# Another order of the q, k and value products, moves one a step, and maxima 13 steps ahead, in a 24-unit attention kernel on one core

## Chip, core and metric

The kernel runs on one core of a Trainium2 chip. The metric is the time of one execution on the device, in microseconds. A profile is one more execution of the same program, recorded by the hardware profiler.

## What is computed

The input x has 4 batches of 1024 tokens with 128 channels, in fp32. Two layers are added to it one after the other, each on a normalised x. The first is a time-mixing layer: three projections, a scan over the tokens (wkv), a gate and a projection back. The second is a chain of six attention cells per batch. Cut to its core:

```python
for c in range(NUM_NOD):                      # 6 cells
    nsrc = min(c + 1, MAX_PREV)
    snode = c - nsrc
    in_q, in_k, in_v = (c - 1, snode, snode + nsrc // 2)
    q = ew[c, 0] * (nodes[in_q] @ We[eq] + be[eq])
    k = ew[c, 1] * (nodes[in_k] @ We[ek] + be[ek])
    v = ew[c, 2] * (nodes[in_v] @ We[ev] + be[ev])
    o = _mha(q, k, v, Wq[c], Wk[c], Wv[c], Wo[c])   # 8 heads of 16 channels, softmax over 1024 keys
    nodes[c] = act_w[c] * o + q
    lind += nsrc
out = _layernorm(nodes[NUM_NOD - 1], ln_g, ln_b)
```

A cell takes q from the cell before it, k and v from older cells. The batches do not depend on each other.

## The kernel before

**Units and steps.** One cell of one batch is a unit, so there are 24. `BATCH_OF` sets their order, with at least three units from a cell to the next of the same batch. A unit has 32 steps: 4 groups (4 heads by 512 queries) of 8 steps, one per 128 keys. Steps are numbered through, s from 0 to 767; r is the step within its unit. In a step TensorE makes

- 4 scores (L496), 128 keys by 512 queries each, into one of three `ring` banks. ScalarE puts exp of each into `e_ring` (L792);
- 2 maxima (`maxima`, L522), 128 queries by 1024 keys each, into the two `wide` buffers in turn, 14 steps (`LOOKAHEAD`) ahead of the scores. Each is reduced by VectorE to one negated maximum per query (L1040). A score and half of a maximum run side by side;
- the weighted sum of values for the step before (`weighted`, L544), in two halves, or in one piece in the second half of a step that also has a product.

Before it writes a wide buffer again, TensorE waits for VectorE to have reduced what was in it:

```python
if w >= 2:
    e.wait_ge(v_mx, w - 1)
```

**The combine.** When the 16 maxima of a group are there (`finished(s)`), VectorE splits them in a high and a low part and transposes them, ahead of the reductions of that step: L1045, L1049 (both tensor_tensor on `max_neg` and `max_part`, in SBUF) and L1058. With `LOOKAHEAD` 14 this is at the start of steps r = 2, 10, 18 and 26. SyncE stores the result to DRAM (`store_rows`) and a step later loads it as extra rows of `q_aug` (`load_rows`), so that the score matmul subtracts the maximum.

**Products.** Some steps hold one product more, in their first half, into a ring bank (`product_of`): two halves of k (`head_k`), of q (`head_q`), of the values (`project_v`) for a coming unit, and two of the output of the unit before (`project_out`, L466 and L471). They stand at r = 1 (q), 5 and 9 (k), 13 and 17 (output), 21 and 25 (values) and 30 (q). ScalarE evicts k, q and output, VectorE copies the values (L935). In the two units after a batch's last cell has run, steps 18 and 19 hold the turns of its result (`final_turn`).

**GpSimd.** Each half of k and of q is split into a rounded high part (cast, L1141) and the rest (tensor_tensor, L1143), both on SBUF. When a part is complete, six DMAs issued by GpSimd (`move_part`, L287) copy it into `q_aug` or `k_aug`; q's go one a step, r = 3 to 8, k's go in two threes at r = 10 and 11. Each waits until the scores of the steps before are done. GpSimd also multiplies the context by the reciprocal denominators (`normalise`, L1159), at r = 11 and after a combine that it waits for (`v_neg`), loads the source of k and values (`load_source`, L317), and at a batch's end applies the last layer norm's scale and shift and adds x (`affine`, L1166 to L1172, from r = 26 in units 20 and 22). Each engine works through its own list in order.

**First layer.** Its stages are spread by the table `MIX_AT` over the lead-in (33 turns, then the steps before step 0, which hold maxima and fillers, `keep_busy`) and over units 0 to 6.

## Time and profile before

| | us |
|---|---|
| median of 3 runs | 2341.45 |
| lowest and highest | 2332.44, 2346.02 |
| profiled execution, its time | 2317.48 |
| its span, first to last instruction | 2315.7 |
| lead-in, until the first score | 114.7 |

The profiled execution's granted TensorE clock was 0.993 of full speed on average. Line numbers, L522 for instance, are those of the kernel before. "Idle before" is the time that an engine stood still ahead of an instruction, and the arrow names what ended it. The ends of matmuls are modelled, so for TensorE the starts are to be compared.

### The profile page before, as it was taken

The page shows a single profiled execution, that of the slowest core. Times are in us where ns is not written, and L with a number is a line of the kernel's source. Part 1 is how long each engine was busy: PE and PEld are TensorE (multiplying, and loading weights), DVE is VectorE, ACT ScalarE, POOL GpSimd, SP SyncE. Part 2 cuts the span into 40 slices and gives each one's busy share as a digit, 9 for nine tenths or more (in the row PEclk, how much of TensorE's full clock was granted, in tenths as well). Part 3 has the DMA queues.
Part 4 walks back from the last instruction along what each step waited for, and adds up shares of the span by engine and source line. Part 5 has one row for each costly group of instructions (what it writes and reads, how often), then busy time and mean ns, then how long its engine had stood idle before and what let it go on. Part 6 is the DMA issues. An engine that isn't in the chain of part 4 may idle for free.

```text
span 2315.7 us, 46444 instructions
## 1 busy us (share of the span) xinstructions
PE 2267.1 (98%) x18079; PEld 865.2 (37%) x18079; DVE 2079.6 (90%) x2259; ACT 1827.2 (79%) x3426; POOL 533.2 (23%) x668
## 2 busy tenths in 40 slices
PE   6999999999999999999999999999999999999996
PEld 3633333333333333333333333333333333333332
DVE  7889899999999999989998999999999999999983
ACT  3267788888887888888888888888888888788785
POOL 5331311322303202212112112112112022321302
PEclk9999999999999999999999999999999999999998
DMA  4230322313313213223223133133134133231201
GB/s 115 61 74 23 80 53 64 79 54 81 77 35 91 65 44 84 62 65 82 58 62 79 53 69 78 35 88 78 31 71 87 29 76 75 52 83 53 65 18 52
DMA packets 86522, 149.40 MB, mean 65 GB/s; under 512 B 34314, under 2 KB 48926, under 8 KB 86302
## 3 DMA queue, kind: packets, MB, share of 16 engines
q0 software_dynamic: 28224, 94.13, 18.2%
q1 hardware_dynamic: 58078, 52.30, 8.7%
q8 instruction: 143, 2.34, 0.4%
q14 instruction: 77, 0.63, 0.1%
HBM read 41.97 MB, written 14.91 MB: 25 GB/s over the span
## 4 chain that ended last, share of the span: by engine, by line
PE 54%; DVE 2%; issue 1%; POOL 0%; ACT 0%; POOLq 0%; ACTq 0%; DVEq 0%
PE ring L496 25%; PE context L544 21%; PE ring L466 1%; DVE max_neg L1040 1%; PE ring L438 1%; PE ring L446 1%; PE ring L471 1%; PE ring L457 1%; PE wide L522 1%; DVE max_part L1045 0%; PE ring L342 0%; DVE stats L827 0%; DVE v_aug L935 0%; POOL k_aug L287 0%; POOL ctxT L1159 0%
## 5 line engine op out<-in xcount | busy, mean ns | idle before, releaser
L1040 DVE TENSOR_REDUCE max_neg<-wide 128x1 f32<-128x1024 f32 x1536 | 1843.4, 1220 | 155.6 <-PE wide L522 150.3
L792 ACT ACTIVATE e_ring<-ring 128x512 f32<-128x512 f32 x3072 | 1668.4, 597 | 320.8 <-PE ring L496 194.2
L496 PE MATMUL ring<-q_aug,k_aug 50*128 50x512 f32 x3072 | 1136.1, 446 | 0.0
L522 PE MATMUL wide<-k_aug,q_aug 48*128 48x512 f32 x3072 | 1122.9, 444 | 7.1 <-DVE max_neg L1040 5.7
L544 PE MATMUL context<-e_ring,v_aug 128*32 128x256 f32 (+1 forms) x10752 | 941.5, 422 | 1.4 <-ACT raw L807 1.4
L496 PEld LDWEIGHTS ring<-q_aug,k_aug 50*128 50x128 f32 x3072 | 463.7, 184 | 755.4 <-ACT e_ring L792 551.1
L522 PEld LDWEIGHTS wide<-k_aug,q_aug 48*128 48x128 f32 x3072 | 458.4, 185 | 31.4 <-DVE max_neg L1040 21.5
L544 PEld LDWEIGHTS context<-e_ring,v_aug 128*32 128x32 f32 x10752 | 211.6, 108 | 481.7 <-issue 367.9
L317 POOL DMA_DIRECT2D src<-node_dram x40 | 23.6, 589 | 685.9 <-PE ring L457 685.9
L1141 POOL CAST q_part<-q_part 128x512 fp32r<-128x512 f32 x47 | 29.0, 617 | 431.3 <-ACT q_part L722 431.2
L287 POOL DMA_DIRECT2D q_aug<-q_part x138 | 71.9, 521 | 189.7 <-PE ring L496 189.7
L698 ACT ACTIVATE node_ring<-ring,col 128x512 f32<-128x512 f32 x48 | 33.0, 688 | 53.6 <-PE ring L471 53.6
L1096 POOL TENSOR_TENSOR rstd<-vareps,neg_half 128x4 f32<-128x4 f32 x24 | 26.1, 1087 | 212.5 <-DVE vareps L836 211.9
L287 POOL DMA_DIRECT2D k_aug<-k_part x138 | 69.3, 510 | 14.2 <-issue 14.0
L1141 POOL CAST k_part<-k_part 128x512 fp32r<-128x512 f32 x47 | 29.1, 620 | 162.0 <-ACT k_part L711 160.8
L1159 POOL TENSOR_TENSOR ctxT<-ctxT,rden_bc 128x1024 f32<-128x1024 f32 x23 | 55.1, 2394 | 36.7 <-DVE max_turn L1058 36.5
L1143 POOL TENSOR_TENSOR k_part<-k_part 128x512 f32<-128x512 f32 x47 | 60.5, 1288 | 3.8
L1143 POOL TENSOR_TENSOR q_part<-q_part 128x512 f32<-128x512 f32 x47 | 60.4, 1285 | 3.9
L471 PE MATMUL ring<-ctxT,w_o 128*128 128x512 f32 x96 | 50.2, 605 | 8.9 <-DVE ctxT L951 8.6
L807 ACT ACTIVATE raw<-context 128x512 f32<-128x512 f32 x96 | 57.9, 603 | 0.6 <-PE context L544 0.5
L466 PE MATMUL ring<-node_ring,w_edge_q 128*128 128x512 f32 x96 | 54.0, 645 | 0.0
L446 PE MATMUL ring<-node_ring,w_q 128*128 128x512 f32 x92 | 51.8, 644 | 0.1
(215 smaller groups left out, 894.2 us busy)
## 6 DMA issues: line engine op xcount, KB each, us to landing
q_aug<-q_part POOLq DMA_DIRECT2D x138, 256.0 KB, 3.7
k_aug<-k_part POOLq DMA_DIRECT2D x138, 256.0 KB, 6.8
src<-node_dram POOLq DMA_DIRECT2D x40, 512.0 KB, 4.9
ctxT<-raw SPq DMA_DIRECT2D x384, 32.0 KB, 2.0
rden_bc<-rden_dram SPq DMA_DIRECT2D x23, 512.0 KB
node_dram<-node_ring SPq DMA_DIRECT2D x16, 512.0 KB, 2.7
q_aug<-rows_dram SPq DMA_DIRECT2D x192, 8.0 KB
node_ring<-in_L_attn_x SPq DMA_DIRECT2D x4, 512.0 KB, 5.2
```

The lines of the kernel that those rows point to most:

```text
L287: e.dma_start(aug[first + slot:first + SPLIT:len(slots), u % 2, :, :], part[parity:P:2, slots[slot], :]).then_inc(signal, DMA)
L446: e.matmul(bk[:, :], w_q[:, c, :], node_ring[:, b, c % 2, half_of(hf)], start=True, stop=True).then_inc(p_qh, 1)
L466: e.matmul(bk[:, :], w_edge_q[:, c, :], node_ring[:, b, c % 2, half_of(hf)], start=True, stop=False)
L471: e.matmul(bk[:, :], w_o[:, c, :], ctxT[:, half_of(hf)], start=False, stop=True).then_inc(p_o, 1)
L496: e.matmul(bk[:, :], k_aug[first:first + AUG, u % 2, h // 2, chunk * P:(chunk + 1) * P].bitcast(F32R), q_aug[first:first + AUG, u % 2, h / ...
L522: done = e.matmul(wide[w % 2][:, half_of(kh)], q_aug[first:first + SPLIT, u % 2, h // 2, q0:q0 + P].bitcast(F32R), k_aug[first:first + SPL ...
L544: done = e.matmul(bank[CTX_BANK][j * VW:(j + 1) * VW, columns], v_aug[:, u % 2, chunk, hg * HG + j, :], e_ring[:, (HG * z + ORDER.index(j) ...
L792: e.activation(e_ring[:, n % E_SLOTS, :], bank[where["st", n]][:, :], ACT.Exp, scale=EXP_SCALE).then_inc(a_exp, 1)
L807: e.activation(raw[:, G % 2, :], bank[CTX_BANK][:, :], ACT.Copy).then_inc(a_cv, 1)
L1040: e.tensor_reduce(max_neg[:, G % 2, row:row + 1], wide[w % 2][:, :], AX_X, ALU.max, negate=True).then_inc(v_mx, 1)
L1141: step(e.tensor_copy(high.bitcast(F32R), x))
L1143: signal(e.tensor_tensor(x, x, high, ALU.subtract), signal_to)
```

## The change

- `LOOKAHEAD` is 13, so the combines are at r = 3, 11, 19, 27, and the lead-in has one step less. One stage of the first layer moves from step -14 to -13.
- k is made at r = 30 and, in the next unit, 1; q at 25 and 5; the values at 9 and 21. For units 1 and 2 they are made late: q at 2 and 3, k at 5 and 9, values at 21 and 22.
- k's moves go one a step at r = 3 to 8, q's at 7 to 12. k's source is loaded at r = 22, the values' source at r = 2.
- `affine` starts at r = 27 and waits for that step's combine; the result is stored at r = 31.

```diff
-LOOKAHEAD = 14
+LOOKAHEAD = 13
...
-        KH_AT, OUT_AT, TURN_AT, V_AT, QH_AT = (5, 9), (13, 17), (18, 19), (21, 25), (30, UC + 1)
+        KH_AT, OUT_AT, TURN_AT, V_AT, QH_AT = (30, UC + 1), (13, 17), (18, 19), (9, 21), (25, UC + 5)
+
+        LATE_KH_AT, LATE_V_AT, LATE_QH_AT = (5, 9), (21, 22), (2, 3)
+
+        SOURCE_AT, V_SOURCE_AT, K_MOVES_AT, Q_MOVES_AT = -10, 2, 3, 7
...
             if u + 1 < LAST:
-                return (19, 22), (20, 23), (21, 24), 26, 30
+                return (19, 22), (20, 23), (21, 24), 27, 31
...
-        def q_steps(u):
+        def unit_steps(u):
             if u in (1, 2):
                 first = UC * (u - 1)
-                return (first + 2, first + 3), first + 5
+                k, q, v = (tuple(first + n for n in at) for at in (LATE_KH_AT, LATE_QH_AT, LATE_V_AT))
+                return k, q, v, [first + 10 + n // 2 for n in range(K_MOVES)], [first + 5 + n for n in range(Q_MOVES)]
             first = UC * (u - 2)
-            return (first + QH_AT[0], first + QH_AT[1]), first + UC + 3
+            k, q = (tuple(first + n for n in at) for at in (KH_AT, QH_AT))
+            v = tuple(first + UC + n for n in V_AT)
+            return (k, q, v, [first + UC + K_MOVES_AT + n for n in range(K_MOVES)],
+                    [first + UC + Q_MOVES_AT + n for n in range(Q_MOVES)])
...
+                if u + 1 < LAST:
+                    e.wait_ge(v_neg, (u + 2) * GPU + 1)
...
+                if half == 0 and 3 <= nxt + 1 < UNITS and r == UC + SOURCE_AT:
+                    load_source(e, nxt + 1, 0)
+                if half == 1 and 3 <= nxt < UNITS and r == V_SOURCE_AT:
+                    load_source(e, nxt, 1)
+                for unit in made_near(s):
+                    k_at, q_at, _, k_moves, q_moves = unit_steps(unit)
+                    if half == 1:
+                        if s in k_at:
+                            split_k(unit, k_at.index(s))
+                        if s in q_at:
+                            split_q(unit, q_at.index(s))
+                    for n in range(K_MOVES):
+                        if k_moves[n] == s and half == 1:
+                            e.wait_ge(p_st, HG * s)
+                            move_k(e, unit, n)
+                    for n in range(Q_MOVES):
+                        if q_moves[n] == s and half == 1:
+                            e.wait_ge(p_st, HG * s)
                             move_q(e, unit, n)
```

The lists of TensorE and ScalarE take the same steps from `unit_steps`.

GpSimd's list in an ordinary unit before, from the q split of step 1 to the source loads (16x4x1024 is one move):

```order
L1141 CAST q_part<-q_part 128x512
L1143 TENSOR_TENSOR q_part<-q_part 128x512
L287 DMA q_aug<-q_part 16x4x1024 x3
L1141 CAST k_part<-k_part 128x512
L1143 TENSOR_TENSOR k_part<-k_part 128x512
L287 DMA q_aug<-q_part 16x4x1024 x3
L1141 CAST k_part<-k_part 128x512
L1143 TENSOR_TENSOR k_part<-k_part 128x512
L287 DMA k_aug<-k_part 16x4x1024 x6
L1159 TENSOR_TENSOR ctxT<-ctxT,rden_bc 128x1024
L317 DMA src<-node_dram 128x1024 x2
```

And with the change, from the k split of step 1 to the last q move (L1156, L1158, L301, L1174 and L331 are the new numbers of L1141, L1143, L287, L1159 and L317):

```order
L1156 CAST k_part<-k_part 128x512
L1158 TENSOR_TENSOR k_part<-k_part 128x512
L331 DMA src<-node_dram 128x1024
L301 DMA k_aug<-k_part 16x4x1024 x2
L1156 CAST q_part<-q_part 128x512
L1158 TENSOR_TENSOR q_part<-q_part 128x512
L301 DMA k_aug<-k_part 16x4x1024 x3
L301 DMA q_aug<-q_part 16x4x1024
L301 DMA k_aug<-k_part 16x4x1024
L301 DMA q_aug<-q_part 16x4x1024 x3
L1174 TENSOR_TENSOR ctxT<-ctxT,rden_bc 128x1024
L301 DMA q_aug<-q_part 16x4x1024 x2
```

One split fewer stands between step 1 and the normalisation (that of step 9), and two q moves now follow the normalisation.

VectorE's list before, from the reciprocal of step 5 to the reductions after step 10's combine:

```order
L988 RECIPROCAL rden_pack<-den_pack 128x64
L1040 TENSOR_REDUCE max_neg<-wide 128x1 x8
L1045 TENSOR_TENSOR max_part<-max_neg 128x2x8
L1049 TENSOR_TENSOR max_part<-max_neg,max_part 128x2x8
L1058 STREAM_TRANSPOSE max_turn<-max_part 128x32
L1040 TENSOR_REDUCE max_neg<-wide 128x1 x16
```

And with the change (L1003, L1055, L1060, L1064 and L1073 are L988, L1040, L1045, L1049 and L1058 before, L949 was L935):

```order
L1003 RECIPROCAL rden_pack<-den_pack 128x64
L1055 TENSOR_REDUCE max_neg<-wide 128x1 x7
L949 COPY v_aug<-ring 128x32x16
L1055 TENSOR_REDUCE max_neg<-wide 128x1 x3
L1060 TENSOR_TENSOR max_part<-max_neg 128x2x8
L1064 TENSOR_TENSOR max_part<-max_neg,max_part 128x2x8
L1073 STREAM_TRANSPOSE max_turn<-max_part 128x32
L1055 TENSOR_REDUCE max_neg<-wide 128x1 x16
```

Between the reciprocal of step 5 and the combine there are now ten reductions, not eight, and the copy of the first values, which came late in the unit before.

## Rows read from the trace of the kernel before

**Rows 1.** The page, part 1: busy us, share of the span, instructions
```profile
PE 2267.1 (98%) x18079; PEld 865.2 (37%) x18079; DVE 2079.6 (90%) x2259; ACT 1827.2 (79%) x3426; POOL 533.2 (23%) x668
```
**Rows 2.** Busy us by stretch: lead-in, units 1 to 6, units 7 to 19
```profile
62.90:114.70 51.80, 51.63 (x228) 32.90 (x228) 45.99 (x80) 11.11 (x44) 18.56 (x19) 0.93 0.16 49
...
223.30:776.30 553.00, 550.53 (x4460) 205.86 (x4456) 507.68 (x541) 450.82 (x837) 126.65 (x162) 1.00 0.28 66
776.30:1930.70 1154.40, 1154.08 (x9573) 428.40 (x9569) 1063.13 (x1028) 966.08 (x1796) 222.22 (x298) 1.00 0.28 65
```
**Rows 3.** Timeline of TensorE (start, us, what), unit 14, starts of steps 18 and 19
```profile
1449.84 0.50 PE L496 MATMUL ring<-q_aug,k_aug 50*128 50x512 f32 x1
...
1452.31 0.49 PE L496 MATMUL ring<-q_aug,k_aug 50*128 50x512 f32 x1
```
**Rows 4.** Timeline of VectorE, unit 23, step 2
```profile
2209.93 0.17 DVE L1045 TENSOR_TENSOR max_part<-max_neg 128x16 fp32r<-128x16 f32 x1
...
2210.55 4.58 DVE L1040 TENSOR_REDUCE max_neg<-wide 128x1 f32<-128x1024 f32 x4
```
**Rows 5.** Timeline of TensorE, unit 23, starts of steps 2 and 3
```profile
2209.10 0.50 PE L496 MATMUL ring<-q_aug,k_aug 50*128 50x512 f32 x1
...
2211.57 0.50 PE L496 MATMUL ring<-q_aug,k_aug 50*128 50x512 f32 x1
2211.80 0.49 PE L522 MATMUL wide<-k_aug,q_aug 48*128 48x512 f32 x1
```
**Rows 6.** Timeline of VectorE, unit 14, step 2
```profile
1404.64 0.78 DVE L1045 TENSOR_TENSOR max_part<-max_neg 128x16 fp32r<-128x16 f32 x1
```
**Rows 7.** Timeline of GpSimd, unit 14, steps 1 and 2
```profile
1404.12 1.28 POOL L1143 TENSOR_TENSOR q_part<-q_part 128x512 f32<-128x512 f32 x1
```
**Rows 8.** Timeline of TensorE, unit 14, start of step 3
```profile
1406.71 0.50 PE L496 MATMUL ring<-q_aug,k_aug 50*128 50x512 f32 x1
1407.12 0.49 PE L522 MATMUL wide<-k_aug,q_aug 48*128 48x512 f32 x1
```
**Rows 9.** Timeline of VectorE, unit 14, step 18
```profile
1450.24 0.17 DVE L1045 TENSOR_TENSOR max_part<-max_neg 128x16 fp32r<-128x16 f32 x1
```
**Rows 10.** Groups by line: busy us, mean ns of one, idle before
```profile
L1045 DVE TENSOR_TENSOR max_part<-max_neg 128x16 fp32r<-128x16 f32 x96 | 42.0, 438 | 2.8
```
**Rows 11.** Timeline of VectorE, unit 20, step 26
```profile
2006.52 2.05 DVE L1045 TENSOR_TENSOR max_part<-max_neg 128x16 fp32r<-128x16 f32 x1
```
**Rows 12.** Timeline of GpSimd, unit 20, first instruction of the affine
```profile
2006.16 2.38 POOL L1166 TENSOR_TENSOR mixing<-mixing,out_g 128x1024 f32<-128x1024 f32 x1
```
**Rows 13.** Timeline of TensorE, unit 20, start of step 27
```profile
2008.41 0.50 PE L496 MATMUL ring<-q_aug,k_aug 50*128 50x512 f32 x1
2010.27 0.50 PE L522 MATMUL wide<-k_aug,q_aug 48*128 48x512 f32 x1 [1.36 <-DVE max_neg L1040]
```
**Rows 14.** Timeline of TensorE, first step of the lead-in's maxima
```profile
62.91 0.70 PE L522 MATMUL wide<-k_aug,q_aug 48*128 48x512 f32 x2 [1.00 <-DMA q_aug<-q_part]
...
64.17 0.73 PE L522 MATMUL wide<-k_aug,q_aug 48*128 48x512 f32 x2
```
**Rows 15.** Timeline of GpSimd, unit 10, the normalisation
```profile
1075.88 2.41 POOL L1159 TENSOR_TENSOR ctxT<-ctxT,rden_bc 128x1024 f32<-128x1024 f32 x1
```
**Rows 16.** Timeline of TensorE, unit 10, step 13, its reader
```profile
1080.56 1.02 PE L471 MATMUL ring<-ctxT,w_o 128*128 128x512 f32 x2
```
**Rows 17.** The 276 moves of L287, from issue to landing
```profile
DMA to landing us min/median/max: 3.5/4.2/11.1
```
**Rows 18.** Timeline of GpSimd, unit 9, k moves
```profile
986.69 2.50 POOL L287 DMA_DIRECT2D k_aug<-k_part x5 [2.85 <-issue]
```
**Rows 19.** Timeline of TensorE, unit 9, step 13
```profile
991.62 1.12 PE L471 MATMUL ring<-ctxT,w_o 128*128 128x512 f32 x2 [0.32 <-POOL ctxT L1159]
```
**Rows 20.** The page, part 6: DMA issues, KB each, median us to landing
```profile
src<-node_dram POOLq DMA_DIRECT2D x40, 512.0 KB, 4.9
```
**Rows 21.** Timeline of SyncE, unit 10, step 10's maxima into q_aug
```profile
1076.90 1.29 SPq L1300 DMA_DIRECT2D q_aug<-rows_dram x2
```

More of the change, by code:

```diff
@@ L225, in build @@
             turns_then_steps((2, 3, 6, 7, 7, 7, 7, 7, 10, 15, 15, 12, 15, 18, 18, 20, 20, 20, 21, 22, 23, 24, 25, 26)),
[L226 removed]
+            turns_then_steps((7, 7, 8, 17, 17, 17, 17, 17, 18, 21, 24, 24, 28, 29, 30, 30, 31, 31, 32), (-13, -13, -12, -12, -9)),
             turns_then_steps((7, 8, 21, 23, 26, 26, 26, 26, 28, 29, 29, 29, 32),
@@ L552, in product_of @@
                 u, r = divmod(s, UC)
-                nxt, prev = u + 1, u - 1
-                if 1 <= nxt < UNITS:
-                    if r in KH_AT:
-                        return lambda: head_k(nxt, KH_AT.index(r), next_bank())
-                    if r in V_AT:
-                        return lambda: project_v(nxt, V_AT.index(r), next_bank())
-                for unit in (nxt, nxt + 1):
-                    if 1 <= unit < UNITS and s in q_steps(unit)[0]:
-                        return lambda: head_q(unit, q_steps(unit)[0].index(s), next_bank())
+                prev = u - 1
+                for unit in made_near(s):
+                    k_at, q_at, v_at, _, _ = unit_steps(unit)
+                    if s in k_at:
+                        return lambda: head_k(unit, k_at.index(s), next_bank())
+                    if s in q_at:
+                        return lambda: head_q(unit, q_at.index(s), next_bank())
+                    if s in v_at:
+                        return lambda: project_v(unit, v_at.index(s), next_bank())
                 if 0 <= prev < LAST:
@@ L733, in stages @@
                 u, r = divmod(s, UC)
-                nxt, prev = u + 1, u - 1
-                if 1 <= nxt < UNITS:
-                    if r in KH_AT:
-                        evict_head_k(nxt, KH_AT.index(r))
-                for unit in (nxt, nxt + 1):
-                    if 1 <= unit < UNITS and s in q_steps(unit)[0]:
-                        evict_head_q(unit, q_steps(unit)[0].index(s))
+                prev = u - 1
+                for unit in made_near(s):
+                    k_at, q_at, _, _, _ = unit_steps(unit)
+                    if s in k_at:
+                        evict_head_k(unit, k_at.index(s))
+                    if s in q_at:
+                        evict_head_q(unit, q_at.index(s))
                 if 0 <= prev < LAST:
@@ L977, in stages @@
                 u, r = divmod(s, UC)
-                nxt, prev = u + 1, u - 1
-                if 1 <= nxt < UNITS:
-                    if half == 0 and r in V_AT:
-                        evict_v(nxt, V_AT.index(r))
+                prev = u - 1
+                for unit in made_near(s):
+                    v_at = unit_steps(unit)[2]
+                    if half == 0 and s in v_at:
+                        evict_v(unit, v_at.index(s))
                 if 0 <= prev < LAST:
@@ L1176, in stages @@
                 nxt, prev = u + 1, u - 1
[L1177 to L1185 removed]
+                if half == 0 and 3 <= nxt + 1 < UNITS and r == UC + SOURCE_AT:
+                    load_source(e, nxt + 1, 0)
+                if half == 1 and 3 <= nxt < UNITS and r == V_SOURCE_AT:
+                    load_source(e, nxt, 1)
+                for unit in made_near(s):
+                    k_at, q_at, _, k_moves, q_moves = unit_steps(unit)
+                    if half == 1:
+                        if s in k_at:
+                            split_k(unit, k_at.index(s))
+                        if s in q_at:
+                            split_q(unit, q_at.index(s))
[5 more added lines that the diff above has]
+                        if q_moves[n] == s and half == 1:
                             e.wait_ge(p_st, HG * s)
                             move_q(e, unit, n)
[L1188 to L1200 removed]
                 if 0 <= prev < LAST:
```

26 lines of the change are left out of this document (3 added, 23 removed).

## The prediction

> **What bounds the kernel now.** I read the busy times first [rows 1]: TensorE is busy for 98% of the span, VectorE for 90%. A busy TensorE may still wait, so I next took the trace by units of 32 steps. The thirteen units 7 to 19 take 1154.4 us, 88.8 each [rows 2], and that repetition lets one unit stand for all. In the timeline of TensorE [rows 3] the thing to look at is when each step starts: a plain one takes 2.46 us (1449.84 to 1452.31), each of its halves 1.23, and TensorE doesn't pause in it. A step with a product, of k, q or values, takes longer by the product.
>
> VectorE has little room beside that. Its reductions, when work has piled up, follow each other every 1.15 us (4.58 for four in [rows 4]), so 2.3 of 2.46 us per step is its own need, and every 8 steps it also combines the maxima of a group (two tensor_tensor and a transpose). The two wide buffers allow it a small delay, and what is beyond that stops TensorE, since maxima(w) waits for reduction w-2. So the question is where the combine stands, and what delays it. The trace has four kinds:
>
> - **Blocked.** At step 2 of unit 14 the combine's first instruction takes 0.78 us [rows 6]; it ends when GpSimd's tensor_tensor of the q split (1404.12 + 1.28) has ended [rows 7]. The next score starts on time at 1406.71, the maxima beside it only at 1407.12 [rows 8]: 0.41 us lost. Step 10, beside the k split, shows the same in each ordinary unit. Over the kernel this instruction took 438 ns on average against 0.17 us for a free one [rows 9, 10]: 96 x 0.268 = 25.7 us, of which two long ones (below) are 3.8; the rest at 0.61 each makes 36 blocked combines.
> - **Free, right behind a product step.** At step 18 of unit 14 the combine starts 0.40 us into the step (1450.24 against 1449.84) and takes 0.17 [rows 3, 9]. The next step starts on time, at 1452.31. Cost: nothing. The product step before it gave VectorE its head start. Step 26 is alike.
> - **Free, with a plain step before it.** This one is rare and carries my forecast. Unit 23 makes no q for a later unit, so its step 1 has no product, and step 2 starts at 2209.10 with VectorE a full 0.83 us behind (2209.93) [rows 4, 5]. Nobody blocks it, yet the score starts at 2211.57 and its maxima at 2211.80: 0.23 us lost.
> - **Behind the output's affine.** In units 20 and 22 GpSimd's 2.38 us tensor_tensor [rows 12] holds step 26's combine for 2.05 us [rows 11], and TensorE goes from 2008.41 to 2010.27: 1.86 us [rows 13].
>
> **The change, part by part.** The number of instructions stays; their places move.
>
> 1. *Combine one step later.* With 13 steps ahead the combines move from steps 2, 10, 18, 26 to 3, 11, 19, 27. The last split before step 3 is that of step 1, which ends about where it does now (1405.40, in step 2), while the combine comes at about 0.83 us into step 3. So none is blocked. But products stay at steps 1, 5, 9, 13, 17, 21, 25, 30, only their kinds change, and none stands at 2, 10, 18 or 26. All four combines become the third kind. An ordinary unit loses 2 x 0.41 = 0.82 now, and 4 x 0.23 = 0.92 after: +0.10. There are 14 (7 to 19, and 21): +1.4 us.
>
> Two combines with a wait that GpSimd caused go away, and that pays for the other two losing their head start. The Trainium skill (SBUF — State Buffer, section Who interferes with whom) says that a tensor_tensor of VectorE with two SBUF inputs waits for a whole GpSimd instruction that reads SBUF. That fits the 0.78; taken alone, it makes the change worth the whole 0.82 a unit, since it knows of no cost for a free combine. The trace of unit 23 disagrees by 0.23 a combine; that case is the first rival.
>
> 2. *Affine behind the combine.* It moves to step 27, behind a wait for that step's combine. Units 20 and 22 lose 0.82 + 1.86 = 2.68 now; after, 3 x 0.23, for their step 19 follows a turn step, which has room. That is -2.0 each, -4.0 us. What is queued behind the affine is the k split of step 30: the affine begins some 1.5 us into step 27 and takes about 7.4, so it ends 1.3 us into step 30, before that split's input is there.
>
> 3. *Lead-in.* One step of maxima fewer comes before the first score. Two half steps of 1.26 us (62.91 to 64.17) go [rows 14]: -2.5 us, as VectorE's two reductions are made later in time that is counted already. Bounds: 0, if the first layer's chain sets the end of the lead-in, and -3.7, a fourteenth of its 51.8 us [rows 2].
>
> 4. *Moves and loads.* Six k moves issued in a row become one a step (steps 3 to 8), the q moves go to 7 to 12. Each issue is about 0.5 us on GpSimd, where there is room. The normalisation stands behind four q moves and before the last two; it may start once step 11's combine is done, about 1.5 us in, and ends 3.9 us in. Its reader starts at 6.8 us into step 11 (two plain steps, 0.23 of waiting, 1.6 within step 13): margin 2.8 us, now 2.3 (1075.88 + 2.41 to 1080.56) [rows 15, 16]. The last q move is issued by step 13; the slowest of 276 landed after 11.1 us [rows 17], and its first reader is step 19, 17 us later. Costed at nothing, covered by that. In unit 9 a pause of 2.85 us between k moves ate the margin [rows 18], and TensorE waited 0.32 us for the normalisation [rows 19]: a single event, -0.3. Source loads are issued 7 or 8 steps ahead of their products, 17 us or more, and land in 4.9 [rows 20]. The maxima of a group travel through DRAM back into q_aug, with one step less for it: in unit 10 that load's second issue ended at 1078.19 [rows 21], and the score of step 16 that wants it comes 7.5 us after step 13's product (1080.56; 2.6 for the rest of step 13 and two plain steps), at 1088.1. Of these 9.9 us 7.4 stay, and these small loads need no longer than the 4.9 of a source of 512 KB. This too is covered.
>
> 5. *First layer's units.* Units 1 to 6 take 553 us, 92.2 each [rows 2], with more work on VectorE and fewer blocked combines. In units 2 and 5 a projection at the end of step 3 will hide step 3's combine (about -0.6 each), elsewhere step 27's free combine starts to cost 0.23. I estimate -1, between -4 (no blocked combine, nothing new) and +3 (two more waits of 0.23 a unit). Unit 0 has many other waits: 0, within 2.
>
> Sum: +1.4 - 4.0 - 2.5 - 0.3 - 1.0 = -6.4 us against the profiled 2317.5. The profiled execution is 24 us below the median shown; I put the difference on that median: 2341.45 - 6.4 = **2335.0**. Its own range takes in the bounds (-14 to +4) and the spread of the runs shown (2332 to 2346): 2321 to 2351.
>
> **Rivals.**
>
> *A, the block was the whole cost.* If a combine in steps 3, 11, 19, 27 costs nothing, the ordinary units give -0.82 x 14 = -11.5, the two affine units -5.4, the first layer's -3, with -2.5 and -0.3: -22.7, **2318.7**. For it: steps 18 and 26 show free combines. Against: their head start comes from steps 17 and 25, and unit 23 shows one without it.
>
> *B, slower: the combine meets GpSimd again.* Place: steps 3 and 11. Point: GpSimd's split of step 1 ends 2.1 us before the combine of step 3 starts, and the first k move is issued in between, from about 0.2 us before step 3 to 0.3 into it; GpSimd must run later by 2.1 us for a split, or 0.5 us for an issue, if issues hold VectorE at all. Price: 0.61 on top of 0.23, twice a unit over 22 units, +26.8: **2361.8**. For it: GpSimd does pause between issues (2.85 us once). Against: it needs that in every unit. This also covers the case that the change doesn't do what it says.
>
> *C, slower: the queue of GpSimd slips.* The normalisation now waits behind ten moves tied to steps. Slips above 2.8 us stop TensorE in step 13; 4.0 a unit would make 1.2 x 22 = +26: 2361.4. Only unit 9 came near.
>
> **Chances.** Forecast 0.66, A 0.20, B 0.08, C 0.06. A measurement of this kernel can tell about 0.5%, 11.7 us, from no change. Of the forecast's own case I count 0.06 as over 0.5% faster, by the spread of the runs. So faster 0.26, same 0.60, slower 0.14. The range reaches to A's time and a little below, and above to the forecast's upper end: 2312 to 2351.
>
> **What would show it.** In the trace of the changed kernel: the combine's first instruction at 0.17 in steps 3, 11, 19 and 27 (mean near 170 ns, not 438); a start 0.83 us into the step; maxima 0.23 late against their score in steps 4, 12, 20 and 28; ordinary units at 88.8; units 20 and 22 near 90; first score near 112 us. It is wrong if those maxima are on time (A, units at 87.9), if some combine still takes 0.78 (B), or if the w_o product of step 13 waits for GpSimd (C).

## The result, and the profile after

The changed kernel is slower. Its four runs have a median of 2393.1 us (2376.25 to 2404.23), the kernel before, on the same chip, 2343.73 us (2332.44 to 2348.32): ratio 1.0253, interval 1.0189 to 1.0316; whether it is slower by more than 2% stays open. Ratios, here and below, leave out runs more than 1.5% above the fastest of their kernel (one of the kernel before, two in experiment 8, one in 10), while the medians and ranges given with them keep these runs. The forecast was 2335.0 and the range ended at 2351.

The profiled execution after took 2394.86 us, its span is 2393.0. The page of the changed kernel (lines as in [rows 1] and after them: busy times, granted TensorE clock in 40 slices, the chain by engine, two groups, two kinds of moves with KB and the median us to landing):

```profile
PE 2309.3 (97%) x18075; PEld 880.5 (37%) x18075; DVE 2048.5 (86%) x2259; ACT 1828.6 (76%) x3426; POOL 531.7 (22%) x668
PEclk9789999899999999999999999999999999999998
PE 76%; DMA 14%; DVE 4%; issue 2%; POOL 2%; SPq 1%; ACT 0%; POOLq 0%; DVEq 0%; ACTq 0%
L485 PE MATMUL ring<-ctxT,w_o 128*128 128x512 f32 x96 | 58.5, 695 | 46.2 <-POOL ctxT L1174 37.6
L1174 POOL TENSOR_TENSOR ctxT<-ctxT,rden_bc 128x1024 f32<-128x1024 f32 x23 | 54.0, 2350 | 217.9 <-DMA rden_bc<-rden_dram 184.3
q_aug<-q_part POOLq DMA_DIRECT2D x138, 256.0 KB, 7.5
k_aug<-k_part POOLq DMA_DIRECT2D x138, 256.0 KB, 5.0
```

VectorE became less busy (2079.6 before), as it should once nobody blocks its combines. But DMA, which had no share in the chain before, now has 14%. L485 is the output product (L471 before), L1174 the normalisation (L1159 before). The normalisation waits for the broadcast reciprocal denominators, `rden_bc`, 184.3 us in all. The view of waits says how often (us in total, times, longest):

```profile
POOL ctxT L1174 <- DMA rden_bc<-rden_dram: 184.3, 22, 10.5
PEld ring L485 <- POOL ctxT L1174: 52.7, 19, 4.1
PE ring L485 <- POOL ctxT L1174: 37.6, 18, 3.2
```

So in nearly every unit GpSimd waits for the denominators, and TensorE for GpSimd. The stretches of the kernel after (us; busy time and instructions of PE, PEld, DVE, ACT, POOL; granted clock; DMA share; GB/s), to be held against [rows 2]: lead-in, 6 us of it, unit 0, units 1 to 6, units 7 to 19:

```profile
62.00:119.00 57.00, 56.92 (x222) 36.25 (x222) 44.46 (x78) 11.12 (x44) 18.55 (x19) 0.78 0.15 44
102.00:108.00 6.00, 6.00 (x17) 3.64 (x16) 3.76 (x7) 0.00 (x0) 0.09 (x1) 0.50 0.00 0
119.00:234.10 115.10, 110.46 (x783) 42.30 (x782) 96.97 (x117) 77.36 (x143) 32.63 (x39) 0.93 0.22 46
234.10:801.20 567.10, 559.64 (x4454) 209.05 (x4450) 504.58 (x541) 451.27 (x839) 128.18 (x164) 0.98 0.29 65
801.20:2003.00 1201.80, 1176.83 (x9572) 435.59 (x9568) 1043.14 (x1028) 966.90 (x1795) 221.24 (x298) 0.98 0.28 62
```

Units 7 to 19 take 92.4 us each instead of 88.8. By steps, the 77.3 us that the span grew come from: step 13 of the units +63.9 (median of the fourteen ordinary units, 7 to 19 and 21, 7.86 us, before 4.24); step 14 +5.4; the lead-in +4.2 and unit 0 +6.5; the combines' steps 3, 11, 19, 27 together -25.6 and the steps behind them +22.5; +0.4 elsewhere. Most of it is step 13.

One unit shows how. Unit 14 starts at 1446.7, its step 11 at 1476.82. First SyncE's queue (start, length) of the kernel after:

```profile
1464.43 1.29 SPq L1338 DMA_DIRECT2D rden_dram<-rden_pack  x2
1471.69 0.64 SPq L1345 DMA_DIRECT2D rden_bc<-rden_dram  x1
```

The same two issues in the kernel before, whose unit 14 starts at 1398.4:

```profile
1416.27 1.29 SPq L1326 DMA_DIRECT2D rden_dram<-rden_pack  x2
1420.90 0.64 SPq L1333 DMA_DIRECT2D rden_bc<-rden_dram  x1
```

The denominators travel to DRAM (**store leg**) and back, spread over the partitions (**load leg**). The store is issued 17.7 to 17.9 us into the unit in both. The load, which waits for the store to land, follows 4.63 us later before and 7.26 after. What GpSimd does meanwhile, after:

```profile
1464.70 1.63 POOL L301 DMA_DIRECT2D k_aug<-k_part  x3
1466.37 0.51 POOL L301 DMA_DIRECT2D q_aug<-q_part  x1
1468.29 0.51 POOL L301 DMA_DIRECT2D k_aug<-k_part  x1 [1.41 <-PE ring L510]
1468.79 0.51 POOL L301 DMA_DIRECT2D q_aug<-q_part  x1
1470.75 0.51 POOL L301 DMA_DIRECT2D q_aug<-q_part  x1 [1.45 <-PE ring L510]
1473.73 0.51 POOL L301 DMA_DIRECT2D q_aug<-q_part  x1 [2.47 <-PE ring L510]
1484.03 2.34 POOL L1174 TENSOR_TENSOR ctxT<-ctxT,rden_bc 128x1024 f32<-128x1024 f32 x1 [9.79 <-DMA rden_bc<-rden_dram]
1486.31 1.05 POOL L301 DMA_DIRECT2D q_aug<-q_part  x2
```

Eight moves of 256 KB are issued beside the two legs, and then GpSimd stands for 9.79 us. The load leg, from the end of its issue (1472.33) to the start of the normalisation, is 11.7 us.

The load has no landing time in these rows, but its packets are on record: in the DMA view of a window the moves are in queue 0, SyncE's transfers in queue 1 (packets, MB, share of 16 engines). After, in the 4.0 us from the end of the load's issue (1472.33 to 1476.37), queue 0 alone is served, and the engines are busy throughout:

```profile
q0 software_dynamic: 185, 0.61, 102.3%
```

Five moves were in flight when the load was issued (before: two). The load's 128 packets of 4 KB run from 1476.4 to 1483.1, and the normalisation starts 0.9 us behind them. In the kernel before, from the end of the load's issue to its last packet (1421.54 to 1427.3), both queues are served:

```profile
q1 hardware_dynamic: 136, 0.52, 36.3%
q0 software_dynamic: 61, 0.18, 10.9%
```

There the first packet comes 0.9 us after the issue, not 4.0, and the last one at 1427.2, 28.8 us into the unit; after, it is 36.4 us into the unit. The 7.6 us between them are 2.5 of a later issue, 3.2 until the first packet and 1.9 of a slower transfer. TensorE after, at that place:

```profile
1482.64 1.12 PE L480 MATMUL ring<-node_ring,w_edge_q 128*128 128x512 f32 x2
1486.42 1.58 PE L485 MATMUL ring<-ctxT,w_o 128*128 128x512 f32 x2 [2.65 <-POOL ctxT L1174]
1487.93 0.79 PE L510 MATMUL ring<-q_aug,k_aug 50*128 50x512 f32 x1
```

It waits 2.65 us, and then its output product takes 1.58 for two (1.02 before, [rows 16]) and a score 0.79 instead of 0.50: the granted clock was 1.00 while it waited and is 0.61 from 1488 to 1491. The wait and the slower products behind it make the 4.5 us by which step 13 of this unit grew (8.70, before 4.24). Where the low clock reaches into step 14, that step grows too, in unit 3 to 6.33 us.

### The profile page after: what moved, and what is told of

Its sections match the earlier page's. It is cut to its first block, busy times and chain, and to the rows that moved or that the text cites. A ratio compares the mean times of both kernels' runs of the same rounds, so it can differ in the third digit from the quotient of the medians.

```text
span 2393.0 us, 46438 instructions
## 1 busy us (share of the span) xinstructions
PE 2309.3 (97%) x18075; PEld 880.5 (37%) x18075; DVE 2048.5 (86%) x2259; ACT 1828.6 (76%) x3426; POOL 531.7 (22%) x668
## 4 chain that ended last, share of the span: by engine, by line
PE 76%; DMA 14%; DVE 4%; issue 2%; POOL 2%; SPq 1%; ACT 0%; POOLq 0%; DVEq 0%; ACTq 0%
PE ring L510 33%; PE context L558 28%; DMA rden_bc<-rden_dram 9%; DMA rden_dram<-rden_pack 5%; PE wide L536 3%; PE ring L485 2%; PE ring L452 2%; DVE max_neg L1055 2%; PE ring L460 2%; POOL ctxT L1174 2%; PE ring L471 1%; PE ring L480 1%; PE context L628 1%; SPq L1338 0%; PE ring L356 0%
## 5 line engine op out<-in xcount | busy, mean ns | idle before, releaser
L1055 DVE TENSOR_REDUCE max_neg<-wide 128x1 f32<-128x1024 f32 x1536 | 1837.4, 1219 | 262.7 <-PE wide L536 258.2
L536 PE MATMUL wide<-k_aug,q_aug 48*128 48x512 f32 x3072 | 1137.2, 449 | 5.7 <-DMA q_aug<-q_part 2.7
L558 PE MATMUL context<-e_ring,v_aug 128*32 128x256 f32 (+1 forms) x10752 | 953.7, 427 | 1.5 <-ACT raw L821 1.4
L510 PEld LDWEIGHTS ring<-q_aug,k_aug 50*128 50x128 f32 x3072 | 470.8, 186 | 771.7 <-ACT e_ring L806 552.5
L536 PEld LDWEIGHTS wide<-k_aug,q_aug 48*128 48x128 f32 x3072 | 464.4, 187 | 26.3 <-issue 10.7
L331 POOL DMA_DIRECT2D src<-node_dram x40 | 23.6, 591 | 467.3 <-PE ring L471 467.3
L1156 POOL CAST k_part<-k_part 128x512 fp32r<-128x512 f32 x47 | 29.1, 620 | 383.6 <-ACT k_part L725 382.4
L1156 POOL CAST q_part<-q_part 128x512 fp32r<-128x512 f32 x47 | 28.9, 615 | 344.8 <-ACT q_part L736 344.6
L485 PE MATMUL ring<-ctxT,w_o 128*128 128x512 f32 x96 | 58.5, 695 | 46.2 <-POOL ctxT L1174 37.6
L1174 POOL TENSOR_TENSOR ctxT<-ctxT,rden_bc 128x1024 f32<-128x1024 f32 x23 | 54.0, 2350 | 217.9 <-DMA rden_bc<-rden_dram 184.3
L301 POOL DMA_DIRECT2D k_aug<-k_part x138 | 71.1, 517 | 92.3 <-PE ring L510 90.2
L301 POOL DMA_DIRECT2D q_aug<-q_part x138 | 71.1, 517 | 87.8 <-PE ring L510 87.1
L1158 POOL TENSOR_TENSOR k_part<-k_part 128x512 f32<-128x512 f32 x47 | 60.5, 1288 | 3.8
L1158 POOL TENSOR_TENSOR q_part<-q_part 128x512 f32<-128x512 f32 x47 | 60.4, 1284 | 4.0
```

What stands on the lines that cost most here:

```text
L301: e.dma_start(aug[first + slot:first + SPLIT:len(slots), u % 2, :, :], part[parity:P:2, slots[slot], :]).then_inc(signal, DMA)
L485: e.matmul(bk[:, :], w_o[:, c, :], ctxT[:, half_of(hf)], start=False, stop=True).then_inc(p_o, 1)
L510: e.matmul(bk[:, :], k_aug[first:first + AUG, u % 2, h // 2, chunk * P:(chunk + 1) * P].bitcast(F32R), q_aug[first:first + AUG, u % 2, h / ...
L536: done = e.matmul(wide[w % 2][:, half_of(kh)], q_aug[first:first + SPLIT, u % 2, h // 2, q0:q0 + P].bitcast(F32R), k_aug[first:first + SPL ...
L558: done = e.matmul(bank[CTX_BANK][j * VW:(j + 1) * VW, columns], v_aug[:, u % 2, chunk, hg * HG + j, :], e_ring[:, (HG * z + ORDER.index(j) ...
L1055: e.tensor_reduce(max_neg[:, G % 2, row:row + 1], wide[w % 2][:, :], AX_X, ALU.max, negate=True).then_inc(v_mx, 1)
```

## The experiments

Theory after the result: **the moves delay the denominators' way through DRAM**, and the rest of the forecast stands. Rivals: the 13 steps of lookahead do it; or GpSimd's queue does (rival C). Each label has its own ratio against runs of the kernel before on the same chip, whose medians were 2332.0 to 2332.1 for experiments 1 to 8 and 2328.9 for 9 and 10. The window of the lead-in is told apart throughout, since its granted clock differs from one execution to another.

The ratios contain the effect of that clock as well. So here is what each profiled execution takes from the start of unit 1 to its last instruction: 2092.3 us before, 2159.0 after, and in experiments 1 to 10 in turn 2089.1, 2089.8, 2097.1, 2085.4, 2089.6, 2180.0, 2092.0, 2073.2, 2170.8 and 2073.2. By this measure the change costs 3.2%, and experiments 1, 2, 5 and 7 are level with the kernel before (within 0.2%), though their ratios lie below 1.

**1. The moves made small.** From unit 3 on each move copies a sixteenth; their number, places and waits stay.

```diff
-            e.dma_start(aug[first + slot:first + SPLIT:len(slots), u % 2, :, :], part[parity:P:2, slots[slot], :]).then_inc(signal, DMA)
+            cols = S if u < 3 else S // 16
+            e.dma_start(aug[first + slot:first + SPLIT:len(slots), u % 2, :, 0:cols], part[parity:P:2, slots[slot], 0:cols]).then_inc(signal, DMA)
```

> The changed kernel, but from unit 3 on each q and k move copies only the first 64 of 1024 columns: the same number of issues and waits, a sixteenth of the bytes (the output is computed from partly stale q and k, so only its time is read). Theory: the moves of steps 5 to 10 keep the DMA engines busy while the denominators go to DRAM and back, so the normalisation comes late and TensorE waits in step 13. Then step 13 of the ordinary units falls from about 7.9 us to 4.24, a unit from 92.8 to 88.8, and the whole by about 75 us, to a ratio near 1.00 against the kernel before. Rival 1, the number or place of GpSimd's issues and not their bytes: step 13 stays near 7.9 us and the ratio near 1.025. Rival 2, SyncE's own queue is late: also no change.

Measured: 2310.96 us (2309.51 to 2324.29, 10 runs), ratio 0.9921 (0.9882 to 0.9959). Span 2307.7, step 13 4.24, units 88.8. The denominators' load is issued 20.3 us into the unit, the normalisation starts at 31.9. In this kernel the DMAs leave out most of q and k, so only its time says something. GpSimd's queue holds the same instructions in the same order as in the changed kernel, so the queue alone is not the cause; the bytes are.

**2. The moves put off, q's and k's.** Same order of products, same 13 steps; k's moves in two threes, q's from step 11, two a step.

```diff
-        SOURCE_AT, V_SOURCE_AT, K_MOVES_AT, Q_MOVES_AT = -10, 2, 3, 7
+        SOURCE_AT, V_SOURCE_AT, K_MOVES_AT, Q_MOVES_AT = -10, 2, 3, 11
...
-            return (k, q, v, [first + UC + K_MOVES_AT + n for n in range(K_MOVES)],
-                    [first + UC + Q_MOVES_AT + n for n in range(Q_MOVES)])
+            return (k, q, v, [first + UC + K_MOVES_AT + n // 3 for n in range(K_MOVES)],
+                    [first + UC + Q_MOVES_AT + n // 2 for n in range(Q_MOVES)])
```

> The changed kernel with all bytes, but the k moves in threes at steps 3 and 4 and the q moves in pairs at steps 11, 12 and 13, so that none is issued between step 5 and the normalisation. Theory (competition for the DMA engines): the normalisation no longer waits for the denominators, step 13 is back at 4.24 us, ordinary units at 88.8, total about 70 to 75 us under the changed kernel; left over against the kernel before are the lead-in and unit 0 (+10.7) less the affine's wait (-4): ratio 1.00 to 1.006. If the last q moves land too late, step 19 waits instead. Rival (the path is late for a reason of its own): ratio stays near 1.025.

Measured: 2324.45 us (2310.22 to 2334.49, 10), ratio 0.9956 (0.9915 to 0.9997); step 13 4.24, units 88.8. With whole moves, at other places, the wait is gone. The ratio fell below the expected 1.00 to 1.006, which had counted the changed kernel's lead-in and unit 0 (+10.7 us) as part of the change. SyncE's queue of this kernel in unit 14:

```profile
1435.82 1.29 SPq L1338 DMA_DIRECT2D rden_dram<-rden_pack  x2
1438.94 0.64 SPq L1345 DMA_DIRECT2D rden_bc<-rden_dram  x1
```

No move is issued beside the store leg here, and it takes 3.12 us from issue to issue. The profiled span (2332.7) holds a lead-in of 132.9 us at a low clock, of which more below.

**3. Only the lookahead.** The kernel before with 13 steps.

```diff
-LOOKAHEAD = 14
+LOOKAHEAD = 13
...
-            turns_then_steps((7, 7, 8, 17, 17, 17, 17, 17, 18, 21, 24, 24, 28, 29, 30, 30, 31, 31, 32), (-14, -13, -12, -12, -9)),
+            turns_then_steps((7, 7, 8, 17, 17, 17, 17, 17, 18, 21, 24, 24, 28, 29, 30, 30, 31, 31, 32), (-13, -13, -12, -12, -9)),
```

> The kernel before with 13 steps of lookahead and nothing else (one stage of the first layer from step -14 to -13). Theory of the combine: no combine of an ordinary unit is blocked, each costs 0.24 us in steps 4, 12, 20, 28, so ordinary units stay at 88.8 us, and step 13 at 4.24, since no q move stands beside the denominators. Theory of the lead-in: if the shorter lead-in alone makes TensorE's clock stay at half for longer, the first score comes near 119 us rather than 114.7 and unit 0 takes some 115 us rather than 108.6; ratio about 1.004. Rival: the lead-in's loss comes from the late products or moves of unit 0; then the first score comes near 112 us, as I had forecast, and the ratio is 0.998 to 1.000.

Measured: 2335.19 us (2316.77 to 2341.45, 10), ratio 1.0013 (0.9979 to 1.0047): no difference. Step 13 stays at 4.24. Steps 3 and 11 take 2.46, and 4, 12, 20 and 28 take 2.70: term 1 of the prediction without its term 4. Term 2 is not in it, since the affine doesn't wait here: in step 27 of units 20 and 22 it still holds the combine, for 1.76 and 1.79 us, and step 28 takes 4.94 and 4.31. Neither theory of the lead-in came true as stated: the first score came at 126.0, at a mean granted clock of 0.73 from 62 us on, and unit 0 took 108.3.

**4. The block alone.** The kernel before, its combines where they were, but the q split of step 1, the k split of step 9 and the affine wait until the combine is done.

```diff
+                if u + 1 < LAST:
+                    e.wait_ge(v_neg, (u + 2) * GPU + 1)
...
+                            if r == 1:
+                                e.wait_ge(v_neg, u * GPU + 2)
...
+                        if r == 9:
+                            e.wait_ge(v_neg, u * GPU + 3)
```

> The kernel before with 14 steps of lookahead, where GpSimd's q split of step 1, its k split of step 9 and the affine of step 26 wait for the combine of step 2, 10 and 26. Theory: the combine keeps the head start of the product step and is not blocked, so it costs nothing: 0.83 us less in each ordinary unit (units at 87.9), 1.86 less in units 20 and 22, in all 15 to 20 us: ratio 0.992 to 0.994. Rival: the splits then come too late for the k moves and the normalisation, and TensorE waits in step 13 instead: ratio 1.00 or above.

Measured: 2310.02 us (2307.6 to 2311.9, 4), ratio 0.9897 (0.9829 to 0.9965). Units 88.1; every step without product is 2.46; no combine is blocked (mean 171 ns). Step 13 grew to 4.50, because GpSimd's queue now runs later and the normalisation starts 34.1 us into the unit: a small piece of rival C. All four runs here are near 2310, the kernel before's lie between 2317 and 2352; of the 1.0% only 0.3% (2085.4 against 2092.3) is found from unit 1 on.

**5. Only the q moves put off.** Of the edit of 2, the q half; k moves stay one a step at 3 to 8.

```diff
-        SOURCE_AT, V_SOURCE_AT, K_MOVES_AT, Q_MOVES_AT = -10, 2, 3, 7
+        SOURCE_AT, V_SOURCE_AT, K_MOVES_AT, Q_MOVES_AT = -10, 2, 3, 11
...
-                    [first + UC + Q_MOVES_AT + n for n in range(Q_MOVES)])
+                    [first + UC + Q_MOVES_AT + n // 2 for n in range(Q_MOVES)])
```

> The changed kernel with the k moves one a step (3 to 8) as changed, and the q moves alone put off, in pairs at steps 11 to 13. Theory, that the number of bytes moved beside the denominators decides: four k moves are issued between the denominators' store (17.7 us into a unit) and 22 us, as q moves were in the kernel before, so the broadcast of the denominators is issued near 22.5 us and not 25.2, lands before step 11's combine, and step 13 is back at 4.24 us; ratio 0.994 to 1.00. Rival: one move a step beside the denominators is enough, whichever it is; then step 13 stays above 6 us.

Measured: 2311.24 us (2309.3 to 2327.05, 10), ratio 0.9916 (0.9881 to 0.995); step 13 4.24, units 88.9. SyncE's queue of this kernel in its unit 14:

```profile
1413.14 1.29 SPq L1338 DMA_DIRECT2D rden_dram<-rden_pack  x2
1420.27 0.64 SPq L1345 DMA_DIRECT2D rden_bc<-rden_dram  x1
```

and GpSimd's:

```profile
1427.50 2.38 POOL L1174 TENSOR_TENSOR ctxT<-ctxT,rden_bc 128x1024 f32<-128x1024 f32 x1 [9.99 <-PE ring L510]
1429.83 3.03 POOL L301 DMA_DIRECT2D q_aug<-q_part  x6
```

I had expected the load leg to be issued earlier. It is not: 7.13 us after the store, as in the changed kernel (7.26). So the store leg is stretched by the k moves: at 1413.41, behind the q split of step 5, GpSimd issues three of them in one burst of 1.63 us, right beside the store. The leg takes 3.12 us with no move beside it (experiment 2), 4.63 with single ones (before) and 7.13 with the burst. But the load has landed by 1427.50, at most 6.6 us after its issue ended, against 11.7 (its last packet is 5.1 us after that end, against 10.8); GpSimd's wait now is for its own step, TensorE's. The four q moves that were issued from step 7 on are worth at least 5 us of the load leg, and without them the later issue does no harm.

**6. The converse.** The kernel before, q moves four steps later (7 to 12).

```diff
-            return (first + QH_AT[0], first + QH_AT[1]), first + UC + 3
+            return (first + QH_AT[0], first + QH_AT[1]), first + UC + 7
```

> The kernel before with its q moves one a step at 7 to 12 instead of 3 to 8, and nothing else. Theory: the denominators' store now goes alone, its broadcast is issued near 20.3 us as in the run without bytes, and only then meets five q moves and three k moves. If the load leg alone matters, the normalisation waits and step 13 takes 6 us or more; if the two legs add up, the earlier issue makes good the slower load, and step 13 stays between 4.24 and 5.5 us. I expect the second. The moves of k, nine in a row with q's at steps 10 to 12, may push the normalisation on GpSimd itself by up to 1 us.

Measured: 2405.45 us (2402.6 to 2422.35, 4), ratio 1.0329 (1.0274 to 1.0384), the slowest of all. Step 13 holds at 4.24, as expected; what it costs elsewhere I did not foresee. The load leg has q moves alone beside it, and no burst before it: the load's last packet comes 6.8 us after its issue in unit 14, 27.8 us into the unit. So it takes both, k's burst and q's moves behind it, to make the normalisation late. Steps 15, 16 and 17 take 4.59, 3.35 and 5.65 in ordinary units. The waits of this kernel:

```profile
PE ring L496 <- DMA q_aug<-rows_dram: 35.5, 18, 3.2
```

The scores of step 16 wait for the rows of maxima, which make the same trip through DRAM. In SyncE's queue the load of the rows follows their store by 6.9 us:

```profile
1457.35 0.54 SPq L1288 DMA_DIRECT2D rows_dram<-max_turn  x1
1464.29 1.30 SPq L1300 DMA_DIRECT2D q_aug<-rows_dram  x2
```

GpSimd issues nine moves and a source load from just before that store on:

```profile
1456.70 0.53 POOL L287 DMA_DIRECT2D q_aug<-q_part  x1
1457.32 2.99 POOL L287 DMA_DIRECT2D k_aug<-k_part  x6
1460.32 2.39 POOL L1159 TENSOR_TENSOR ctxT<-ctxT,rden_bc 128x1024 f32<-128x1024 f32 x1
1462.66 1.05 POOL L287 DMA_DIRECT2D q_aug<-q_part  x2
1463.70 0.56 POOL L317 DMA_DIRECT2D src<-node_dram  x1
```

This reads as the same mechanism on another victim, though no run takes the bytes away here. The moves of one operand, moved by four steps in the otherwise unchanged kernel, cost 3%, or 4.2% from unit 1 on (2180.0 against 2092.3).

**7. The denominators two steps earlier**, with the change's moves as they are.

```diff
-                    if half == 1 and r == 5:
+                    if half == 1 and r == 3:
...
-                        if r == 6:
+                        if r == 4:
```

> The changed kernel with all its moves where they are, but VectorE takes the reciprocals of the denominators in step 3 instead of 5, and SyncE stores and broadcasts them in step 4 instead of 6. Theory: the wait of step 13 is that path's lateness, 3 to 5 us; five us earlier it is gone: step 13 at 4.24 us, ordinary units 88.8 to 89.2 (the reciprocal now falls into the step of the combine, up to 0.4 us more), ratio 0.996 to 1.00. Rival, something in steps 7 to 12 holds the broadcast whenever it is issued: step 13 stays above 6 us.

Measured: 2313.67 us (2311.68 to 2327.36, 9), ratio 0.993 (0.9892 to 0.9969). The load is issued some 16.4 us into the unit and step 13 is 4.24; step 5 pays 0.2 for the reciprocals beside the reductions, so units take 89.1. The ratio is a little below the expected 0.996 to 1.00; from unit 1 on this kernel is level with the one before. Moving the victim works as well as moving the moves.

**8. The block alone, normalisation first.** Experiment 4, and the normalisation of step 11 goes ahead of that step's k moves.

```diff
+                if 0 <= prev < LAST and half == 0 and r == 11:
+                    normalise(prev)
                 if 1 <= nxt < UNITS and half == 0 and r == 11:
...
-                    if half == 0 and r == 11:
-                        normalise(prev)
```

> The kernel before with the splits and the affine waiting for the combine (as in splits_wait), and the normalisation of step 11 ahead of the last three k moves instead of behind them. Theory: the 0.26 us that splits_wait still lost in step 13 (4.50 against 4.24) goes, ordinary units fall from 88.1 to 87.9 us, the total by about 5 us, unit 9's single event included; ratio 0.985 to 0.992. Rival: the last k moves land after step 18 begins, and TensorE waits there for as much.

Measured: 2297.02 us (2294.33 to 2329.14, 6), ratio 0.9844 (0.9789 to 0.9898): with 10, which only adds fillers, the fastest kernel of this study. The ratio flatters it: from unit 1 on it takes 2073.2 us against 2092.3, 0.9% less, and its fastest run is 1.0% below the fastest of the kernel before (2294.3 against 2316.6). The instruction view of its combine (ns min/median/max), and GpSimd's q split behind it, in the timeline:

```profile
L1045 DVE TENSOR_TENSOR max_part<-max_neg x96: 110/174/177, 91.2 to 2233.3; 128x16 fp32r<-128x16 f32 x96
```

```profile
1396.50 0.61 POOL L1141 CAST q_part<-q_part 128x512 fp32r<-128x512 f32 x1 [8.30 <-DVE max_turn L1058]
```

The split waits for the combine's end (L1058), none of 96 combines is above 177 ns, step 13 is back at 4.24 and a unit takes 87.9. Here the block's whole price, 2 x 0.41 a unit, is won, and no head start is given up: steps 1, 9, 17 and 25 still hold products ahead of the combines of 2, 10, 18 and 26.

**9. The change's order with 14 steps.** The last rival for step 13.

```diff
-LOOKAHEAD = 13
+LOOKAHEAD = 14
...
-            turns_then_steps((7, 7, 8, 17, 17, 17, 17, 17, 18, 21, 24, 24, 28, 29, 30, 30, 31, 31, 32), (-13, -13, -12, -12, -9)),
+            turns_then_steps((7, 7, 8, 17, 17, 17, 17, 17, 18, 21, 24, 24, 28, 29, 30, 30, 31, 31, 32), (-14, -13, -12, -12, -9)),
```

> The changed kernel with 14 steps of lookahead again (all else as changed). Theory of the combine, in places where no kernel had it yet: combines are at steps 2, 10, 18, 26. Step 10's now stands behind a product of values, no split beside it: free, so step 11 takes 2.46 us. Step 26's stands beside the q split of step 25, as step 2's beside the k split of step 1: both blocked at 0.78 us, and steps 3 and 27 take 2.87. Steps 4, 12, 20 and 28 are at 2.46. The theory of the denominators says that the lookahead has nothing to do with step 13: it stays at 7 to 8.5 us. Rival: the shorter lookahead made the denominators late; then step 13 is at 4.24.

Measured, in a single execution: 2392.95 us, step 13 8.29, and the waits of this kernel read like the changed one's:

```profile
POOL ctxT L1174 <- DMA rden_bc<-rden_dram: 177.9, 20, 10.4
PEld ring L485 <- POOL ctxT L1174: 58.0, 20, 4.3
PE ring L485 <- POOL ctxT L1174: 42.1, 19, 3.5
```

The lookahead has no part in step 13. The combine's first instruction is back at a mean of 415 ns, and steps 4, 12, 20 and 28 at 2.46.

**10. A busier TensorE in the lead-in.** Experiment 8 with fillers around the output's bias products, one place where the lead-in's clock falls.

```diff
+                    keep_busy(BANK)
                     out_biases()
+                    keep_busy(BANK)
```

> The fastest kernel so far (splits_wait_norm_first) with one filler matmul of 512 columns ahead of and one behind the 12 one-column bias matmuls of the lead-in. In the profile of the kernel before the granted clock is half from 98.2 us, just behind them, and its runs stand in groups at 2318, 2330 and 2348 us. Theory: these nearly empty matmuls let the clock fall; fed from both sides it stays up, and all runs lie at 2296 to 2300 us (about 2 us of fillers added), none at 2329. Rival: the fall comes from the waits around them or from elsewhere; then runs at 2329 and above stay as frequent as in splits_wait_norm_first (2 in 6).

Measured: 2296.29 us (2294.54 to 2332.17, 8), ratio 0.9838 (0.9787 to 0.9888), like 8. Two of the eight runs are still long, 2324 and 2332 us, as the rival said. In the profiled execution, the longest, the clock fell before the bias products, at 77.9 us, and the first score came at 143.9. The theory of the trigger fell; what makes the clock fall there stays open.

## Why the prediction was wrong

**The step that failed is 4, "Moves and loads … Costed at nothing".** It let the normalisation start "once step 11's combine is done" and gave it a margin of 2.8 us. It asked when GpSimd is free and when the moves land, and never when the normalisation's other input lands. The broadcast denominators have no landing time among the DMA issues, and I left them out of the list of what it waits for instead of asking for a bound. There was one: the load is issued 22.5 us into the unit and the normalisation starts at 32.5, so it took at most 9.4 us from the end of its issue. The packets in the trace of before say more: the last one is 28.8 us into the unit, so the load had 3.7 us to spare, and 3.1 with the normalisation due at 31.9. My margin held only if it landed in time, which I had not asked. The change brought q's moves from steps 3 to 8 to 7 to 12, onto just that stretch, and k's into the store leg. In unit 14 the last packet came 7.6 us later, the normalisation began at 37.3 instead of 31.9, and of these 5.4 us late the margin of 2.8 took up its part: 2.6 were left, and TensorE waited 2.65. Experiments 1, 2, 5 and 7 each remove the wait by another way (fewer bytes, other places, only q's places, an earlier start), 3 and 9 clear the lookahead, and 1 clears GpSimd's queue. Price: 63.9 + 5.4 us in steps 13 and 14.

**Rival C had the place, not the mechanism.** "The w_o product of step 13 waits for GpSimd" is what happened, but GpSimd was not late: it stood still for 9.8 us. The price, 1.2 a unit, was too low; it is 2.9 (63.9 over 22 units), wait and lower clock together.

**Term 1, the combine: right.** After, a combine with a plain step before it costs 0.24 (2.70 against 2.46; forecast 0.23), and its first instruction is free:

```profile
1476.82 0.49 PE L510 MATMUL ring<-q_aug,k_aug 50*128 50x512 f32 x1
1479.28 0.50 PE L510 MATMUL ring<-q_aug,k_aug 50*128 50x512 f32 x1
1479.53 0.49 PE L536 MATMUL wide<-k_aug,q_aug 48*128 48x512 f32 x1
```

(TensorE after, step 11 of unit 14 and the start of step 12: the maxima come 0.25 behind their score.) In VectorE's timeline of the same kernel the combine starts 0.83 us into that step, as forecast:

```profile
1477.65 0.17 DVE L1060 TENSOR_TENSOR max_part<-max_neg 128x16 fp32r<-128x16 f32 x1
```

Its mean over 96 is 191 ns (438 before, [rows 10]); two are blocked, not 38. Rivals A and B fall with that. The Trainium skill (SBUF — State Buffer, section Who interferes with whom) gives VectorE's tensor_tensor a wait for the whole GpSimd instruction; experiments 4 and 8, where only that overlap was taken away, agree with 0.17 in place of 0.78.

**Term 2, the affine: right.** Steps 27 of units 20 and 22 take 2.46 us, 1.86 less each, and in experiment 1, without the wait of step 13, these units take 2.2 and 2.8 us less than before (forecast 2.0). Experiment 4 has the affine's wait at its old place with the same step of 2.46; experiment 3, without the wait, shows the block moved to step 28.

**Term 3, the lead-in: right in kind, swamped by the clock.** The nearest pair in clock is experiment 9, with 14 steps, whose first score comes at 112.7 us with 0.97 granted from 62 us on, and experiments 1 and 5, with 13, at 110.2 with 0.96: the forecast 2.5 us. The 114.7 of before (0.94) hold some clock besides, and experiment 4, with 14 steps and 1.00, has 110.9. But the profiled execution after had 0.78, and its first score came at 119.0.

**Term 5 and the sum.** Where the moves do no harm, units take 88.8 to 88.9 (forecast 88.8). The span of experiment 1 is 2307.7, 8.0 below before's 2315.7; the forecast sum was -6.4. Part of that is luck: 4.5 of the 8.0 are the lead-in with its clock (forecast 2.5), and from unit 1 on it is 3.2 less against a forecast of 3.9. With that said, terms 1, 2, 3 and 5 would have been near for a kernel whose moves stood elsewhere. The range's bounds of -14 and +4 were wider than the terms' own add up to (-12.6 and +2.1). And term 4 had a second unasked trip, that of the maxima, which "need no longer than the 4.9": in the change it did no harm, in experiment 6 TensorE waited for it.

## What to carry to other kernels

Before a bulk transfer is moved, write down for every wait near its new place all that it waits for, and give each of these a latest landing; one whose landing the trace doesn't list is bounded by the waiter's start, and better by its packets in the DMA view of a window, queue by queue; the slack that this leaves is what the move may use up. Round trips through DRAM that an engine waits for (here denominators and rows of maxima) should have no bulk transfer issued beside them, or start early enough. And where a port is contested, it was cheaper here to let the idle engine wait for the busy one (three `wait_ge` and the normalisation put first, 0.9% from unit 1 on) than to reorder the program around it. Last, where one stretch differs by chance from execution to execution, compare the others without it: four runs that happened to be good made 0.3% look like 1.0% in experiment 4.

## What the runs showed of the hardware

**Transfers on different queues delay each other far below full load.** Units 7 to 19 of the changed kernel use the DMA engines at a mean share of 0.28, and yet a load of 512 KB takes 11.7 us with five moves of 256 KB in flight at its issue, and at most 6.6 with one (unit 14 of the changed kernel and of experiment 5). The q moves, too, land later, after 7.5 us (median) instead of 3.7; k's, no longer six in a row, land after 5.0 instead of 6.8. The mean share hides that in the few microseconds that count the 16 engines are full: 102.3% by the view's count in the 4.0 us before the load's first packet, all of it for GpSimd's queue. The Trainium skill (DMA: Bandwidth & Descriptors, section Queues, rings and completion order) says that each DMA engine takes its queues in turn and changes only after a whole packet, which there is several descriptors. The 4.0 us with one queue alone served would fit a long turn, but the page gives no time for it, and no run here tests it.

**TensorE's granted clock in the lead-in differs from one execution to the next, and I can't say why.** The lead-in's windows (columns as above) of two kernels whose lead-ins hold the same work; first of the kernel with only q's moves put off:

```profile
62.00:110.20 48.20, 47.57 (x220) 30.68 (x220) 43.76 (x79) 11.10 (x44) 18.51 (x19) 0.96 0.18 54
```

then of the kernel with both moves put off:

```profile
62.00:132.90 70.90, 68.89 (x220) 44.81 (x220) 46.10 (x80) 11.10 (x44) 18.88 (x20) 0.64 0.14 41
```

The same 220 matmul records take 48 or 69 us. In the changed kernel TensorE is granted 0.50 from 102 to 119 us, although it counts as busy throughout (the 6.00 of 6.00 above). One plain consequence: runs of one and the same kernel lie up to 38 us apart. The profiled spans of experiments 8 and 10 differ by 34.6 us, and all of it is in the lead-in and unit 0 (29.7 and 4.9); from unit 1 on both take 2073.2. Single profiled spans, then, must be compared without these two. I had not expected this of stretches in which TensorE does not pause, and 10 did not find the cause.
